# Rotary attention of an eight-layer kernel: a part of the row maxima moved from VectorE to ScalarE and GpSimd

## What is computed

```python
q = (x @ Wq + bq).reshape(bsz, seq, H, HD).transpose(0, 2, 1, 3)
k = (x @ Wk + bk).reshape(bsz, seq, H, HD).transpose(0, 2, 1, 3)
v = (x @ Wv + bv).reshape(bsz, seq, H, HD).transpose(0, 2, 1, 3)
q = q * cos + _rotate_half(q) * sin
k = k * cos + _rotate_half(k) * sin
scores = jnp.einsum('bhqd,bhkd->bhqk', q, k) / sqrt(HD)
attn = jax.nn.softmax(scores, axis=-1)
ao = jnp.einsum('bhqk,bhkd->bhqd', attn, v)
x1 = _layernorm(x + ao @ Wo + bo, g1, be1)      # then a mixture of experts
```

## Time and profile before

| | us |
|---|---|
| median of 3 runs | 5788.23 |
| lowest and highest | 5783.87, 5794.31 |
| profiled execution, its own time | 5795.58 |
| profiled execution, its span | 5793.8 |
| rotary stage, first value matmul to last row of the ring banks | 2614 to 3395 |
| TensorE, VectorE, ScalarE, GpSimd busy, share of the span | 91%, 71%, 47%, 21% |

### The profile page before, as it was taken

One profiled execution on the slowest core, in us unless ns is written; L12 is line 12 of the kernel. 1 busy time (PEld: TensorE's weight loads), 2 busy tenths in 40 slices (PEclk: granted clock), 3 DMA queues, 4 the chain that ended last, 5 costly groups with the idle time before them and its releaser, 6 DMA issues. The chain is left out here.

```text
span 5793.8 us, 86268 instructions
## 1 busy us (share of the span) xinstructions
PE 5261.2 (91%) x31277; PEld 2629.9 (45%) x31277; DVE 4089.6 (71%) x7068; ACT 2696.3 (47%) x4526; POOL 1227.6 (21%) x859
## 2 busy tenths in 40 slices
PE   6999998787999999989999978899898899997999
PEld 2333333344567777772222248333333333334676
DVE  7888886774677777768898944677787877763412
ACT  4656665221233333337776756444344344442333
POOL 0110100220112322321102203244343233331000
PEclk7999998787989999999999999999999999998999
DMA  4211110002111111112111122000000000001000
GB/s 88 46 31 30 31 30 11 0 0 61 36 33 23 37 23 30 25 23 38 31 31 34 39 60 78 26 16 16 12 19 9 12 12 12 12 12 37 5 4 8
DMA packets 148359, 156.96 MB, mean 27 GB/s; under 512 B 48980, under 2 KB 95108, under 8 KB 147508
## 3 DMA queue, kind: packets, MB, share of 16 engines
q1 hardware_dynamic: 143336, 142.37, 11.3%
q0 software_dynamic: 4096, 8.40, 0.5%
q10 hardware_dynamic: 504, 0.69, 0.1%
HBM read 118.20 MB, written 37.40 MB: 27 GB/s over the span
## 5 line engine op out<-in xcount | busy, mean ns | idle before, releaser
L3946 DVE TENSOR_REDUCE wide_max_parts<-wide_p 128x2 f32<-128x1024 f32 x496 | 592.9, 1218 | 127.9 <-PE wide_p L3915 117.8
L759 ACT ACTIVATE attn_w<-l_p 128x512 f32<-128x512 f32 x1024 | 549.3, 596 | 276.0 <-DVE l_p L1203 152.0
L2518 PE MATMUL caus_p<-caus_x_one,big 128*128 128x129 f32 x4608 | 642.7, 287 | 0.0
L610 DVE TENSOR_REDUCE l_max_parts<-l_p 128x2 f32<-128x1024 f32 x512 | 602.1, 1219 | 46.8 <-PE l_p L586 42.4
L2602 ACT ACTIVATE big<-caus_p 128x512 f32<-128x512 f32 (+3 forms) x768 | 345.9, 489 | 576.7 <-PE caus_p L2504 418.5
L610 DVE TENSOR_REDUCE rot_max_parts<-rot_p 128x2 f32<-128x1024 f32 x488 | 574.1, 1219 | 51.1 <-PE rot_p L586 48.6
L2518 PEld LDWEIGHTS caus_p<-caus_x_one,big 128*128 128x128 f32 x4608 | 592.8, 199 | 35.7 <-issue 2.6
L4213 PE MATMUL wide_p<-arena 64*128 64x512 f32 x2048 | 538.0, 604 | 0.0
L4348 ACT ACTIVATE attn_w<-wide_p 128x1024 f32<-128x1024 f32 x342 | 350.4, 1024 | 390.6 <-PE wide_p L4213 387.1
L4144 POOL TENSOR_TENSOR big<-big,attn_w 128x1024 f32<-128x1024 f32 x128 | 333.5, 2606 | 454.5 <-PE wide_p L3915 442.2
L610 DVE TENSOR_REDUCE caus_max_parts<-caus_p 128x2 f32<-128x1024 f32 (+2 forms) x360 | 340.5, 956 | 24.2 <-PE caus_p L586 15.9
(11 more groups left out here) (625 smaller groups left out, 8957.4 us busy)
## 6 DMA issues: line engine op xcount, KB each, us to landing
arena<-q_parts SPq DMA_DIRECT2D x576, 32.0 KB
arena<-k_parts SPq DMA_DIRECT2D x576, 32.0 KB
arena<-inverse_rows SPq DMA_DIRECT2D x64, 256.0 KB
l_q_stack<-q_parts SPq DMA_DIRECT2D x279, 32.0 KB
l_k_stack<-k_parts SPq DMA_DIRECT2D x279, 32.0 KB
q_parts<-arena SPq DMA_DIRECT2D x8, 768.0 KB, 3.6
k_parts<-arena SPq DMA_DIRECT2D x8, 768.0 KB, 3.6
attn_w<-moe_in SPq DMA_DIRECT2D x19, 256.0 KB
```

Of the source, the lines that this page charges most:

```text
L610: self.nc.vector.tensor_reduce(self.max_parts[:, 2 * p:2 * p + 2, n, half], pair[:, :, 0:self.width(n, half)], AX.X, ALU.max).then_inc(*se ...
L759: self.nc.scalar.activation(self.exps[t % len(self.exps)], bank, ACT.Exp).then_inc(*self.exped.up())
L2518: mm = nc.tensor.matmul(outs[o % 2][:, nq % 2 * (C + 1):(nq % 2 + 1) * (C + 1)], exps[h % 2][:, kb, nq * P:(nq + 1) * P], x_one[b % 2][:, ...
L3946: self.nc.vector.tensor_reduce(self.max_parts[:, :, n, h], side, AX.X, ALU.max).then_inc(*self.maxed.up())
```

## The change

Of each unit from the second on, score tiles 3, 9, 19 and 25 are set **aside**: 60 in the stage. For such a tile ScalarE copies the pair of banks (128 by 1024) into one of two rooms in SBUF. GpSimd halves the room twice; each halving takes the larger of two numbers a and b as max(a - b, 0) + b, three instructions, the first time over 512 and the second time over 256 numbers per partition. VectorE reduces the 256 that are left of the 1024 (`late_on_dve`), six score tiles (three steps) later, and no longer reads the tile itself. The bank pair is free when ScalarE has copied it. A room is taken again when VectorE has reduced what was in it two asides ago. So that there is room in `big`, `v_tok` holds two batches instead of four (columns 4T to 6T), and the rooms are columns 6T to 8T. The values of batch 2 and 3 wait on VectorE until GpSimd has filled `v_one` from the batch whose place they take.

```diff
     def values_on_dve(self, v, b, half, bank):
         i = HALF * b + half
         v.wait_ge(*self.v_multiplied.at(i + 1))
-        self.nc.vector.tensor_tensor(self.values[2][:, 4 * i:4 * i + 4, :], banks4(bank),
+        at = 4 * i % self.values[2].shape[1]
+        self.nc.vector.tensor_tensor(self.values[2][:, at:at + 4, :], banks4(bank),
                                      spread(self.values[1], 4), ALU.add).then_inc(*self.v_kept.up())
...
+    LAG = 6
...
+        for i, tile in enumerate(self.tiles):
+            if self.is_aside(len(self.tiles) * u + i):
+                steps[i + self.LAG] = [("late", u, len(self.tiles) * u + i, *tile)] + steps[i + self.LAG]
         return steps
+
+    def is_aside(self, o):
+        return o >= len(self.tiles) and o % len(self.tiles) in self.aside
...
+    def max_left(self, o):
+
+        n = self.asides(o)
+        return (self.aside_kept, n + 1) if self.is_aside(o) else (self.maxed, o - n + 1)
...
+    def aside_on_act(self, a, o, pair):
+        k = self.asides(o)
+        a.wait_ge(*self.max_scored.at(o + 1))
+        if k >= len(self.room):
+            a.wait_ge(*self.aside_maxed.at(k - len(self.room) + 1))
+        self.nc.scalar.copy(self.room[k % len(self.room)][:, :, :], pair).then_inc(*self.aside_kept.up())
+
+    def aside_on_pool(self, pool, o):
+        k, nc = self.asides(o), self.nc
+        room = self.room[k % len(self.room)]
+        pool.wait_ge(*self.aside_kept.at(k + 1))
+        for i, wide in enumerate((BANK // 2, BANK // 4)):
+            one, other, done = room[:, :, 0:wide], room[:, :, wide:2 * wide], self.halved
+            if i:
+                pool.wait_ge(*done.at(6 * k + 3))
+            nc.gpsimd.tensor_tensor(one, one, other, ALU.subtract).then_inc(*done.up())
+            pool.wait_ge(*done.at(6 * k + 3 * i + 1))
+            nc.gpsimd.tensor_scalar(one, one, 3e38, 0.0, ALU.min, ALU.max).then_inc(*done.up())
+            pool.wait_ge(*done.at(6 * k + 3 * i + 2))
+            nc.gpsimd.tensor_tensor(one, one, other, ALU.add).then_inc(*done.up())
+
+    def late_on_dve(self, v, new, u, o, p, n, half):
+        k, left = self.asides(o), HALF * u + n // (NT // HALF)
+        v.wait_ge(*self.halved.at(6 * (k + 1)))
+        if new(self.joined, left):
+            v.wait_ge(*self.joined.at(left))
+        self.nc.vector.tensor_reduce(self.max_parts[:, 2 * p:2 * p + 2, n, half],
+                                     self.room[k % len(self.room)][:, :, 0:BANK // 4], AX.X,
+                                     ALU.max).then_inc(*self.aside_maxed.up())
...
-                maxima = [step for step in now if step[0] in ("max", "join")]
+                maxima = [step for step in now if step[0] in ("max", "late", "join")]
...
-                               first_slot=units_before % PairBuffers.SLOTS)
-        self.v_tok = core.big[:, 4 * T:4 * T + nb * T].rearrange("p (n c) -> p n c", c=C)
+                               first_slot=units_before % PairBuffers.SLOTS, aside=(3, 9, 19, 25))
+        self.v_tok = core.big[:, 4 * T:6 * T].rearrange("p (n c) -> p n c", c=C)
...
+                    b = args[0]
+                    if b > 1 and new(weighted.filled, GROUPS * (b - 1)):
+                        v.wait_ge(*weighted.filled.at(GROUPS * (b - 1)))
                     proj.values_on_dve(v, *args, bank)
```

32 lines of the change are left out of this document (26 added, 6 removed).

## The result

The changed kernel takes 5800.07 us (median of 22 runs, 5786.1 to 5816.56), the kernel before 5789.43 us beside it. The ratio is 1.0022 with a 95% interval of 1.0014 to 1.0029: some 13 us slower, between 8 and 17; the medians lie 10.6 apart. (The ratio compares the runs without one of the kernel before that took 20559.22 us.) I had forecast 27.6 us more. The direction holds and the time lies inside the range, but the sum is more than twice too large. The change is also just over 0.2%, about where a measurement of this kernel begins to tell two versions apart.

The account below looks back on a forecast made before the run. TensorE's written order was taken as the bound in most steps, VectorE close behind. Terms -6 + 22.5 + 8.7 + 2.4 = +27.6 on the median of 5788.2 gave 5815.8 us, 0.48% slower; range 5792 to 5832.

Parts of the forecast that it names:

- copies beside a keep: Steps 8 and 0: the copy delays the keep, so TensorE's fourth exp score waits; 21 x 0.77 = 16.2 us.
- copies without one: Steps 5 and 13: the copy delays exponential 2, so TensorE's second exp score is late; 21 x 0.3 = 6.3 us.
- late reduces beside the join: Steps 11 and 3: TensorE's second score tile of the next step is 0.38 us late, 23 times; +8.7, 0 to 14.
- fill stall: Two batches: TensorE's weighing waits 1.2 us for the fill, behind tile 19's halvings on GpSimd; +2.4 us, 0 to 10.
- units 4, 8, 9 and 10: Late stretches, where a batch is normalised: a lighter VectorE gains there; -6 us, from 0 to -12.
- What bounds the kernel: Rotary stage: TensorE's written order bounds most steps, VectorE only where a batch is normalised, costing some 35 us in all.
- The rival in which VectorE is the bound: Rotary stage: VectorE bounds and ScalarE's copy hides; 5776 us, or 5741 if every step gained; chance 0.08.
- that of a late GpSimd: Tiles over 7.4 us on GpSimd make every late reduce wait, and TensorE behind it; 5850 us at 8 us; chance 0.13.
- The one in which the costs mostly hide: ScalarE's catch up at half price, late reduces in gaps, relief at -12: +2 to +8, 5793 us; chance 0.12.
- ScalarE's term: ScalarE's copies can't be hidden in their steps and make TensorE's exp scores late: +22.5 us, bounds 11.5 to 32.
- My lower bound, 11.5 us: Price of ScalarE's copies at 0.15 and 0.4 us each, with the semaphore free and the copy overlapping its neighbours more.
- the clock as a rival of the whole stage: TensorE's clock falls more often as it pauses in plain steps too; eight more falls +24, 5840 us; chance 0.12.

Follow-up runs that it names:

- the early fill: The changed kernel with the fill of a unit's values into v_one moved to step 4 of the unit before: ratio 1.0029 to before, stage 776.2 us.
- the 11 tiles: The changed kernel with only 11 tiles set aside, in units 5, 9, 10 and 11, where VectorE was late: ratio 0.9981 to before, stage 764.9 us.

## Why the prediction was right in sign and wrong in size

The difference of after to before, summed by place from the distances of the weighings. The rows of copies and late reduces leave out units 4, 8, 9 and 10, whose whole difference stands in a row of its own:

| term | forecast | measured |
|---|---|---|
| copies beside a keep | 21 x 0.77 = 16.2 | 18 places, 9.2 |
| copies without one | 21 x 0.3 = 6.3 | 18 places, 2.6 |
| late reduces beside the join | 23 x 0.38 = 8.7 | 20 places, 4.9 |
| fill stall | 2 x 1.2 = 2.4 | 6.0, of which 2.7 is the clock |
| units 4, 8, 9 and 10 | -6 | -6.5 (-10.1 against before's second profile) |
| sum | +27.6 | +16.1 (+12.4) |

**What bounds the kernel** was right: with VectorE's tiles dropped outright the plain units stay at 43.2. The rival in which VectorE is the bound is refuted, and that of a late GpSimd too (idle before line 651: 0.0). The one in which the costs mostly hide is refuted as a whole, since the plain units pay 1.83 each; but the part of it that gave ScalarE's catch up half of my price came true, and the kernel's 10.6 to 13 us lie nearer to its +2 to +8 than to my 27.6.

**The step that failed is the size of ScalarE's term**, 22.5 forecast and 11.8 measured, some 13 with the copies in units 4, 8 and 10. The plain unit, which no clock touches, says it most plainly: I had forecast 2 x 0.3 + 2 x 0.77 = 2.14 us for its copies, and the run with the copies added shows 1.17. The places were right: 21 + 21 forecast; 18 + 18 found outside units 4, 8, 9 and 10, and three more with a keep inside them (behind step 0 of units 4, 8 and 10, 0.49 to 0.55). The wait was right: TensorE's exp score for exponential 2, and with the keep its fourth exp score. The price was a chain of four starts, 0.54 for each exponential and 0.96 for the copy, from which a small slack was taken at the end. Each link was 0.05 to 0.07 too long (two exponentials take 0.97 and not 1.08, the copy 0.89), so that exponential 2 starts 0.18 earlier than I had it. Of my 0.29 this leaves 0.11; exponential 2 lasts 0.63 and not 0.60, and the score was due 0.02 earlier, which gives the 0.16 in TensorE's row. In the distance of two weighings that is 0.06 alone and 0.15 behind a late reduce; and with the keep it is 0.53, not 0.77. The start-to-start of the exponentials when ScalarE doesn't wait could have been read from before: four of them take 2.07 us and not 2.18 when nothing holds them up. My lower bound, 11.5 us, had been worked out from just this ("the copy overlapping its neighbours more") and came out near the value, in part by chance: its 0.4 for a copy with a keep is 0.53.

**The late reduces** cost 0.24 each by these places, not 0.38: 0.32 behind the reduce, of which 0.09 comes back in the next distance, that of the send. I had not followed the step behind. Where a copy follows, the 0.09 is lost again (0.15 behind it and not 0.06), so that from the run with the halvings to the changed kernel a plain unit grows by 0.66, 0.33 for each late reduce. By that count the late reduces were mis-sized little, and the copies are nearly the whole miss of a plain unit (0.97 of 1.07). The rule "free where it stands in for a tile" was right, and the run with tiles 3 and 19 shows its price where it doesn't: 0.33.

**The fill stall** was right in its place, its cause and the tile. It was 1.67 and not 1.2, and a second cost follows it that I had left out: a half clock behind TensorE's pause, 1.30 and 1.35 us more in the two batches, in both profiles of after. It is no fixed price of such a pause: of the eight stalls of this length in four profiles (two of after, one with the halvings, one with tiles 3 and 19) five have the fall behind them and three don't. I had the clock as a rival of the whole stage ("TensorE pauses in plain steps too") and gave it 0.12; in plain units it stays at 1.00. It belonged, with a chance of its own, to the one place with a pause of over a microsecond.

**The relief** was given as -6 and came out near that, but by another account. Those units hold their own copies and late reduces too, and dropping the tiles outright is worth -10.9 to -14.5 there. The -6.5 therefore holds some 1.5 us of copies and about 1 of late reduces too, and its nearness to my -6 is luck. My -6 left the clock out; the fall at 3102.9 and the one at 3133.6 that before shows in both its profiles are in neither of after's, and that is part of it. How much I can't say, since a shorter step and a missing fall come together.

**The range** of 5792 to 5832 doesn't follow from the bounds given: the low ends of the four terms add up to -0.5 us and the high ends to +56, from 5788 to 5844, and I had written no rule by which it is narrower.

What stays open: the runs with the copies, the halvings and the early fill are 7 us slower by the ratio than by their stage, and the 11 tiles 9 us faster. The profiles can't settle it: outside the rotary stage, where the work is the same, the fourteen of them range from 5014.4 to 5040.1 us. No run was made on that.

There remain the two rules of the Trainium skill that the prediction weighed. The first tensor_scalar of the stage, which is the first of the whole trace, starts 0.09 us behind the end of the subtraction before it, in GpSimd's timeline of after:

```profile
2622.77 1.27 POOL L640 TENSOR_TENSOR big<-big 128x512 f32<-128x512 f32 x1 [14.30 <-ACT big L630]
2624.13 0.61 POOL L642 TENSOR_SCALAR big<-big 128x512 f32<-128x512 f32 x1
```

By the rule of the Trainium skill's GPSIMD Engine Reference (section 2.1, Instruction dispatch) a first call of freshly loaded code would have cost some 6 us there; it cost nothing, so either nothing was loaded there or the rule doesn't hold for this instruction. And the late reduces, which read SBUF, take 403 to 414 ns all sixty. Only 22 of them run beside a GpSimd that is busy for more than half of their time, and those take no longer than the others, so the shared port of which the Trainium skill's Perfetto Trace Analysis (Optimizing Scalar/DVE Operations) warns shows in none of them.

## What to carry to other kernels

An engine that is the bound in a few stretches and not elsewhere is worth relieving in those stretches alone: dropping four tiles in each of 15 units took nothing from the plain ones, while copying them cost each of these 1.2 us. Where a slack of some tenths is subtracted from a chain of starts, take each link from a row in which the engine doesn't wait: here 0.05 to 0.07 in each of three links came near to doubling the answer. And give a fall of the clock behind a new pause of TensorE a price and a chance (here 1.3 us, five times in eight), and profile the same kernel twice before a difference of 1% of a stage is read as the edit's: here the same kernel differed by up to 7.5 us in 757.

## What the runs showed of the hardware

- Steps in which the granted clock is the same repeat to the hundredth: 255 distances of after within 0.02 us in two profiles; of before, where two falls lasted otherwise, 242 of 255 within 0.05.
- TensorE's granted clock fell to half for 3.4 us right behind a pause of 1.6 us at the fill, in both batches of both profiles of after (1.30 and 1.35 us lost). With the halvings added it did so at one of two pauses of that length, and with tiles 3 and 19 at neither. In unit 9 a fall begins behind the same weighing in all fourteen profiles, where the kernel before has 6.9 us between two weighings; it lasted 3.4 us in one profile of before and 13.7 in the other, 4.7 us lost in three steps.
- A tensor_scalar with two operations on GpSimd takes 612 ns for 512 and 399 ns for 256 numbers per partition, about half of a tensor_tensor (1269 and 725).
- On ScalarE, a copy of 128 by 1024 from PSUM that lasts 1020 ns in its row holds the next instruction up for 0.89 us; exponentials of 128 by 512 follow one another at 0.48 to 0.49 us in before's second row of ScalarE in the earlier trace rows, though each lasts 0.60 to 0.63.
